# Softmax denominators of an attention block turned and summed on the vector engine instead of the tensor engine

## What is computed

```python
xn = layernorm(x)                                   # (1, 2048, 128)
q, k, v = xn @ Wq, xn @ Wk, xn @ Wv                 # 16 heads x 64
attn = softmax((q @ k.T) * 64 ** -0.5, axis=-1)
a = (attn @ v).reshape(1, 2048, 1024) @ Wo + bo
e = argmax(softmax(xn @ router_w.T))                # one expert a token
f = square(relu(xn @ expert_fc[e])) @ expert_proj[e].T
out = x + a + f
```

## Time and profile before

| | |
|---|---|
| median of 3 runs | 1392.12 us (1388.15 to 1392.15) |
| profiled execution, its own time | 1389.63 us |
| its span, first to last instruction | 1387.9 us |
| busy PE, DVE, ACT, POOL | 98%, 78%, 53%, 81% |
| DMA engines, mean busy share | 20.3% (SP's queue) |
| mean granted clock of TensorE | 0.993 of 2.4 GHz |

### The profile page before, as it was taken

One profiled execution on the slowest core, in us unless ns is written; L12 is line 12 of the kernel. 1 busy time (PEld: TensorE's weight loads), 2 busy tenths in 40 slices (PEclk: granted clock), 3 DMA queues, 4 the chain that ended last, 5 costly groups with the idle time before them and its releaser, 6 DMA issues.

```text
span 1387.9 us, 20006 instructions
## 1 busy us (share of the span) xinstructions
PE 1365.8 (98%) x6447; PEld 866.1 (62%) x6447; DVE 1078.0 (78%) x1468; ACT 735.2 (53%) x1316; POOL 1121.8 (81%) x908
## 2 busy tenths in 40 slices
PE   7899999999999999999999999999999999999997
PEld 4566666566665666666766666656667666656644
DVE  7987887786787767777777777778677777788877
ACT  4465455565464554554644645545546446556543
POOL 7779997777787877877878877879777788789995
PEclk8999999999999999999999999999999999999998
DMA  4241113220132201331113311123112231111000
GB/s 104 58 120 41 37 41 70 70 67 20 43 89 57 60 19 43 94 69 44 34 39 84 73 40 43 43 71 90 24 42 55 64 79 26 24 23 33 11 19 23
DMA packets 65255, 72.38 MB, mean 52 GB/s; under 512 B 9024, under 2 KB 38272, under 8 KB 65152
## 3 DMA queue, kind: packets, MB, share of 16 engines
q1 hardware_dynamic: 64128, 69.01, 20.3%
q0 software_dynamic: 1024, 2.10, 0.5%
HBM read 17.83 MB, written 5.11 MB: 17 GB/s over the span
## 4 chain that ended last, share of the span: by engine, by line
PE 93%; DVE 2%; POOL 1%; DMA 1%; issue 1%; SPq 1%; ACT 1%; POOLq 0%; DVEq 0%; ACTq 0%
PE OB L1116 31%; PE SB L1062 17%; PE SB L1069 16%; PE MB L1088 15%; PE XB L1153 2%; PE XB L1144 2%; PE XB L1162 2%; PE XB L1050 1%; PE XB L1043 1%; POOL acc L505 1%; DVE mx L767 1%; PE XB L1123 1%; PE XB L1125 1%; PE XB L1124 1%; DMA K<-low 1%
## 5 line engine op out<-in xcount | busy, mean ns | idle before, releaser
L505 POOL TENSOR_TENSOR acc<-acc,ex 128x512 f32<-128x512 f32 x717 | 915.9, 1304 | 99.9 <-DVE acc L790 40.4
L767 DVE TENSOR_REDUCE mx<-MB 128x1 f32<-128x512 f32 x992 | 655.9, 688 | 228.9 <-PE MB L1088 224.1
L619 ACT ACTIVATE ex<-SB 128x512 f32<-128x512 f32 x1024 | 607.2, 599 | 329.8 <-PE SB L1069 262.0
L1116 PE MATMUL OB<-ex,V 128*64 128x512 f32 x2048 | 452.7, 594 | 0.0
L1062 PE MATMUL SB<-Q,K 128*128 128x512 f32 x1024 | 421.9, 412 | 0.5 <-ACT ex L619 0.5
L1069 PE MATMUL SB<-Q,K 128*128 128x512 f32 x1024 | 399.8, 390 | 0.8 <-DMA Q<-mrow 0.8
L1088 PE MATMUL MB<-K,Q 128*128 128x512 f32 x992 | 389.1, 392 | 1.6 <-DVE mx L773 0.6
L1116 PEld LDWEIGHTS OB<-ex,V 128*64 128x64 f32 x2048 | 143.9, 137 | 284.3 <-issue 273.0
L1062 PEld LDWEIGHTS SB<-Q,K 128*128 128x128 f32 x1024 | 192.6, 188 | 96.5 <-issue 53.5
L790 DVE TENSOR_TENSOR acc<-acc,ex 128x512 f32<-128x512 f32 x179 | 205.0, 1145 | 13.5 <-ACT ex L619 1.0
L1088 PEld LDWEIGHTS MB<-K,Q 128*128 128x128 f32 x992 | 186.1, 188 | 46.7 <-DVE mx L767 5.0
(11 more groups left out here) (136 smaller groups left out, 608.8 us busy)
## 6 DMA issues: line engine op xcount, KB each, us to landing
Q<-high SPq DMA_DIRECT2D x124, 128.0 KB, 2.3
K<-high SPq DMA_DIRECT2D x112, 128.0 KB, 2.3
Q<-low SPq DMA_DIRECT2D x64, 128.0 KB, 2.4
K<-low SPq DMA_DIRECT2D x56, 128.0 KB, 2.3
w<-fc SPq DMA_DIRECT2D x23, 256.0 KB, 2.7
w<-projT SPq DMA_DIRECT2D x23, 256.0 KB, 3.1
sorted_x<-res SPq DMA_DIRECT2D x1, 1472.0 KB, 6.9
tok<-sorted_x SPq DMA_DIRECT2D x23, 64.0 KB, 1.7
```

The costliest lines, as they stand in the source:

```text
L505: pool.tensor_tensor(a[:, :], src[:, :], EX[h][ex_slot(kt)][:, :], ALU.add).then_inc(done, 1)
L619: act.activation(EX[h][ex_slot(kt)][:, :], SB[bank_of(n, 2 * kt + h)][:, :], ACT.Exp).then_inc(a_e[h], 1)
L767: dve.tensor_reduce(mx[:, m % 2, u:u + 1], MB[bank_of(m, i)][:, :], AX.X, ALU.max).then_inc(v_m, 1)
L1116: mm = pe.matmul(OB[own[h], :], V[(n // JB) % 2][:, k, own[h]], EX[h][ex_slot(k)][:, :], start=(k == 0), stop=(k == NT - 1))
```

## The change

The three jobs named leave TensorE. DVE's transpose works in squares of 32 x 32: of a 128 x 512 tile each square is turned in its place.

- Denominators. At kt 0 of block n DVE turns both `acc` tiles of block n - 1 by squares and sums each square's row (`fold_sums`), which gives `part` [128, 2 x 16]: sums over groups of 32 keys. SP's `gather_parts` brings the four groups side by side with four DMAs; DVE adds them at kt 3 (`sum_parts`), inverts 32 x 32 numbers at kt 4 (`invert`), turns them at kt 5 (`turn_row`). SP stores the result to DRAM, waits, and reads it back laid over 64 partitions a head (`spread_rd`). `normalise` waits for those DMAs.
- Maxima. `nm` is a 128 x 32 tile (8 columns used) turned by DVE at kt 12, or after the first unit in the opening (`turn_max`); `place_max` has four DMAs a head instead of one.
- Tokens. SP loads the tile with the squares already exchanged, in four DMAs instead of one; DVE turns each square at kt 3, behind `sum_parts`. `expert_up` waits for DVE.

The diff, cut to its core:

```diff
-AT_DEN, AT_KV, AT_Q, AT_WO, AT_NM, AT_T = 8, (1, 9), 5, 13, 11, 12
-AT_INV, AT_ON = 8, 10
+AT_KV, AT_Q, AT_WO, AT_NM, AT_T = (1, 9), 5, 13, 11, 12
+AT_FOLD, AT_SUM, AT_INV, AT_RD, AT_ON = 0, 3, 4, 5, 10
...
+        turned = rd
+        part, parts = sb("part", [P, SQ]), sb("parts", [SQ, P // SQ, SQ])
+        den, inv, row = sb("den", [SQ, SQ]), sb("inv", [SQ, SQ]), sb("row", [SQ, SQ])
...
                 def place_max(m):
                     k = m % QS
-                    wait(sp, a_nm, m.times(1, 1))
+                    wait(sp, v_mrow, m.times(1, 1))
                     wait(sp, g_z, 4 + 2 * QS if m.off else 4)
                     for h in range(2):
-                        copy(Q2[k][h][maxrow[h], :], mrow[h * TB:(h + 1) * TB, :], d_nm[k])
+                        row = Q2[k][h][maxrow[h], :].rearrange("o (q j a) -> o q j a", q=TB, a=SQ)
+                        for j in range(P // SQ):
+                            copy(row[:, :, j, :], mrow[j * SQ + h * TB:j * SQ + (h + 1) * TB, :], d_nm[k])
+
+                def gather_parts(n):
+                    wait(sp, v_part, n.times(2, 2))
+                    for j in range(P // SQ):
+                        sp.dma_start(parts[:, j, :], part[j * SQ:(j + 1) * SQ, :]).then_inc(d_parts, 16)
+
+                def spread_rd(n):
+                    wait(sp, v_row, n.times(1, 1))
+                    wait(sp, d_rd, n.times(32))
+                    sp.dma_start(rows_rd.rearrange("h (t b) -> (h t) b", b=SQ), row[:, :]).then_inc(d_row, 16)
+                    wait(sp, d_row, n.times(16, 16))
+                    for h in range(2):
+                        sp.dma_start(rd[own[h], :], rows_rd[h:h + 1, :].to_broadcast([DH, QB])).then_inc(d_rd, 16)
 
                 def load_tile(r):
...
-                    sp.dma_start(tok[:, :], sorted_x[bass.ds(r.place(P), P), :]).then_inc(d_tile, 16)
+
+                    rows = sorted_x[bass.ds(r.place(P), P), :].rearrange("(i a) d -> a i d", a=SQ)
+                    for j in range(P // SQ):
+                        sp.dma_start(tok[j * SQ:(j + 1) * SQ, :].rearrange("a (i b) -> a i b", b=SQ),
+                                     rows[:, :, j * SQ:(j + 1) * SQ]).then_inc(d_tile, 16)
...
                     for kt in range(NT):
                         for m in q_jobs(n, kt):
                             spread_q(m)
+                        if kt == AT_SUM - 1 and n.off:
+                            gather_parts(n - 1)
+                        if kt == AT_RD and n.off:
+                            spread_rd(n - 1)
...
                 def normalise(n):
-                    wait(pool, v_rd, n.times(2, 2))
-
+                    wait(pool, d_rd, n.times(32, 32))
...
+                def turn_max(m):
+
+
+                    wait(dve, v_nm, m.times(1, 1))
+                    if not (m.i is None and m.off == 0):
+                        old = m - 1
+                        wait(dve, d_nm[old % QS], (old // QS).times(MD, MD))
+                    dve.transpose(mrow[:, :].bitcast(F32), nm[:, :].bitcast(F32)).then_inc(v_mrow, 1)
...
+                def turn_tokens(r):
+                    wait(dve, d_tile, r.times(TD, TD))
+                    wait(dve, t_up, r.times(1))
+                    dve.transpose(tokT[:, :], tok[:, :]).then_inc(v_tok, 1)
...
-                def invert(n, part):
-                    cols = slice(part * QB // 2, (part + 1) * QB // 2)
-                    wait(dve, a_den, n.times(1, 1))
-                    dve.reciprocal(rd[:, cols], rd[:, cols]).then_inc(v_rd, 1)
+                def fold_sums(n):
+
+
+                    for h in range(2):
+                        wait(dve, sums[h][n % 2], added(n, NT - 1))
+                        if h == 0:
+                            wait(dve, g_on, n.times(1))
+                            wait(dve, d_parts, n.times(64))
+                        else:
+                            wait(dve, v_part, n.times(2, 1))
+                        dve.transpose(turned[:, :], acc[h][n % 2][:, :]).then_inc(v_turn, 1)
+                        wait(dve, v_turn, n.times(2, h + 1))
+                        dve.tensor_reduce(part[:, h * QB // SQ:(h + 1) * QB // SQ], turned[:, :].rearrange("p (t k) -> p t k", k=SQ),
+                                          AX.X, ALU.add).then_inc(v_part, 1)
+
+                def sum_parts(n):
+                    wait(dve, d_parts, n.times(64, 64))
+                    dve.tensor_reduce(den[:, :], parts[:, :, :].rearrange("b j c -> b c j"), AX.X, ALU.add).then_inc(v_den, 1)
+
+                def invert(n):
+                    wait(dve, v_den, n.times(1, 1))
+                    dve.reciprocal(inv[:, :], den[:, :]).then_inc(v_inv, 1)
+
+                def turn_row(n):
+                    wait(dve, v_inv, n.times(1, 1))
+                    wait(dve, d_row, n.times(16))
+                    dve.transpose(row[:, :], inv[:, :]).then_inc(v_row, 1)
...
-                        if kt == AT_INV and not start:
-                            invert(n - 1, 0)
-                            invert(n - 1, 1)
+                        if not start:
+                            if kt == AT_FOLD:
+                                fold_sums(n - 1)
+                            if kt == AT_SUM:
+                                sum_parts(n - 1)
+                            if kt == AT_INV:
+                                invert(n - 1)
+                            if kt == AT_RD:
+                                turn_row(n - 1)
...
+                        if has_tile(n) and kt == AT_TOK:
+                            turn_tokens(n - TILE0)
...
-                def denominators(n):
-                    take_spare(a_den, n.times(1, 1))
-                    for h in range(2):
-                        wait(pe, sums[h][n % 2], added(n, NT - 1))
-                    for h in range(2):
-                        mm = pe.matmul(XB[own[h], :], ones[:, 0:DH], acc[h][n % 2][:, :], start=True, stop=True)
-                    mm.then_inc(t_den, 1)
-
```

More of the change, by code:

```diff
@@ L169, in layer @@
         OB, XB = bank("OB"), bank("XB")
[L173 to L180, removed]
+        t_s, t_m, t_pv, t_q, t_k, t_v, t_den, t_wo = (
+            sem(f"t_{n}") for n in ("s", "m", "pv", "q", "k", "v", "den", "wo"))
+        a_e, a_o, a_q, a_k, a_w, a_v = (
+            [sem("a_e0"), sem("a_e1")], *(sem(f"a_{n}") for n in ("o", "q", "k", "w", "v")))
+        v_m, v_nm, v_mrow, v_q, v_k, v_w, v_rd, v_y = (
+            sem(f"v_{n}") for n in ("m", "nm", "mrow", "q", "k", "w", "rd", "y"))
         sums = [[sem(f"sum{h}_{k}") for k in range(2)] for h in range(2)]
@@ L193, in layer @@
         d_sort = [sem(f"d_sort{k}") for k in range(2)]
[L196 to L197 removed]
+        d_tile, v_tok, t_up, t_down, a_up, a_res, g_hid, d_res, d_back, v_back = (
+            sem(n_) for n_ in ("d_tile", "v_tok", "t_up", "t_down", "a_up", "a_res", "g_hid", "d_res",
                                "d_back", "v_back"))
@@ L203, in layer @@
         v_y0 = sem("v_y0")
+        v_turn, v_part, v_den, v_inv, v_row, d_parts, d_row, d_rd = (
+            sem(n_) for n_ in ("v_turn", "v_part", "v_den", "v_inv", "v_row", "d_parts", "d_row", "d_rd"))
         d_out = sem("d_out")
-        QD, KD = 6 * 16, 6 * 16
+        TD = (P // SQ + 2) * 16
+        QD, KD, MD = 6 * 16, 6 * 16, 2 * (P // SQ) * 16
         def unit(n, kt, h):
@@ L646, in kv @@
                                        ACT.Copy).then_inc(a_v, 1)
[L648 to L653, removed]
                 def take_o(n):
@@ L753, in one @@
                             high_q(m)
[L754 to L757, removed]
                 schedule(act, first, one, lambda: take_o(Lin(NB - 1)))
@@ L948, in one @@
                             minus_max(n + 1)
+                        if kt == AT_T and before(n, NB - 1):
+                            turn_max(n + 1)
                         if kt in AT_KV and before(n, NB - JB):
@@ L1032, in ranks @@
                     pe.matmul(XB[:, NT * E:2 * NT * E], ones[:, :], chosen, start=True, stop=True).then_inc(t_rk, 1)
-                def turn_tokens(r):
-                    take_spare(a_tok, r.times(1, 1))
-                    wait(pe, d_tile, r.times(48, 48))
-                    pe.transpose(XB[:, 0:P], tok[:, :], ident[:, :]).then_inc(t_tok, 1)
                 def expert_up(r):
                     take_spare(a_up, r.times(1, 1))
-                    wait(pe, a_tok, r.times(1, 1))
+                    wait(pe, v_tok, r.times(1, 1))
                     for c in range(NC):
@@ L1066, in low_scores @@
                     if kt == 0 and h == 0:
-                        wait(pe, d_nm[k], (n // QS).times(32, 32))
+                        wait(pe, d_nm[k], (n // QS).times(MD, MD))
                         wait(pe, d_one[par], 32)
@@ L1164, in project @@
                     mm.then_inc(t_wo, 1)
-                def turn_max(m):
-                    take_spare(a_nm, m.times(1, 1))
-                    wait(pe, v_nm, m.times(1, 1))
```

(10 more changed lines are left out.)

31 lines of the change are left out of this document (13 added, 18 removed).

## The result

The changed kernel takes 1551.8 us (1549.4 to 1554.4) against 1390.7 before: ratio 1.116, interval 1.113 to 1.119. It is 161 us slower, where 1520 was forecast and 1430 to 1600 held. The span of the profiled execution is 1552.7 us, TensorE's mean granted clock 0.951 (0.993 before).

The account below looks back on a forecast made before the run. TensorE was taken as the bound. 1389.6 - 34.5 freed + 63.6 (stall A) + 3.9 (the opening) + 69.4 (stall B) + 1 (token turn) = 1493.0; with 27 for the clock 1520 us, range 1430 to 1600.

Parts of the forecast that it names:

- The bound: Whole kernel: only TensorE has no room, busy 1278.95 of 1280 us, so its waits are added in full.
- the opening: Start of the kernel: the maxima's eight issues let TensorE go on at 48.7 instead of 44.87, 3.9 us.
- stall A: Next block's first low product: TensorE waits for maxima behind SP's eight issues, 2.05 us x 31 = 63.6 us.
- Freed, 0.92 us a block: Denominators leaving TensorE, between last maximum product and PV batch: 28.5 us over 31 blocks, of 34.5 freed in all.
- DVE at kt 0: Two turns and two reductions of 128x512 add 2.8 us, hidden under 5.05 us; the wait for POOL hidden too.
- the rival of a turn at the reciprocal's pace: DVE turns at kt 0 take 3.4 us each, 96 us more, about 1610; chance 0.03.
- Stall B: Token product: gathers behind SP's K copies delay DVE, 5.4 us x 12 blocks plus 4.6 in block 1, 69.4 us.
- The clock: TensorE's clock falls in about 8 of stall B's 13 blocks, 3.4 us each: 27 us, bounds 0 and 66.
- rival 4: Stall A costs TensorE's clock as well: 53 to 105 us more, about 1600; chance 0.09.

Follow-up runs that it names:

- the kernel before with eight DMAs: Kernel before the change, its maxima laid by eight DMAs of 32 queries instead of two of 128, turn still on TensorE: 1447.5 us, ratio 1.043.
- the denominators alone: Kernel before plus only the change's denominators' part, partial sums gathered ahead of the first K copies; maxima and tokens stay on TensorE: 1379.7 us, ratio 0.993.
- The repaired whole change: Changed kernel with partial sums gathered before the first K copies, maxima turned in kt 11 and copied before the second K copies: 1393.6 us, ratio 1.004.
- the owners' step was moved away: The denominators alone, plus tokens turned on DVE ahead of the partial sums' sum, and block 3's owners' step at kt 7, not kt 0: 1369.2 us, ratio 0.985.
- the gather ahead: Changed kernel with SP gathering the partial sums ahead of the first K copies instead of behind them: 1457.1 us, ratio 1.048.
- denominators alone, gather behind: The denominators alone, but with the partial sums gathered behind the first K copies, as in the changed kernel: 1449.5 us, ratio 1.043.

## Why the prediction was right, and where its sizes were off

**The bound.** TensorE is the bound, and its waits are added in full: right, and somewhat more than in full, as the kernel before with eight DMAs shows (0.35 us beyond each idle). Its idle time in the span went from 22.1 us to 158.7, by 136.6; the prediction's stalls and the opening were 137. That this is so close is partly chance: stall A came out 5 us smaller, and 4.7 us in block 3 were not forecast.

**Freed, 0.92 us a block.** The undisturbed blocks with the denominators alone gave 0.85 to 0.90. The repaired whole change, which sheds more, gained only 0.40 a block between the same two starts (927.0 us against 935.9), with small waits at tokens and maxima in many blocks.

**DVE at kt 0.** The turn of 128x512 takes 0.711 us where 0.69 was taken from the nearest row, and it is hidden in the middle blocks; the rival of a turn at the reciprocal's pace is out. The Trainium skill's 311 ns for a turn of 128x128 in bf16 ("VectorE: DVE Perf Modes", The three transpose paths) is near the 290 ns that this trace shows in float32. What the step missed: it judged POOL by one middle block. After indirect DMAs POOL is late, and the wait for its last add, put at nothing, stops TensorE together with the owners' step of 3.7 us behind it: 4.7 us in block 3 of the changed kernel and 6.5 in the denominators alone, but 2.2 where the owners' step was moved away.

**Stall A.** 62.4 us in 31 waits against 63.6 and 3.9. The issue was the 0.63 of the earlier trace rows less a little (0.573 median over 256); a wait is mostly 1.75 us, not 2.05. In seven blocks it is 2.1 to 3.6 us, and it is so in seven blocks with the gather ahead too, so the other stall isn't the reason; what is stays open. The kernel before with eight DMAs confirms the term without the rest of the change.

**Stall B.** 65.5 us in 12 waits against 64.8, 4.6 in block 1 against 4.6. Its mechanism was right to the queue; the experiments add that it doesn't need the tokens, which only lengthen it from 3.5 us to 5.4.

**The clock** is the term that was mis-sized: 27 us forecast, some 50 measured. The prediction put a fall behind about 8 of the 13 long idles at 3.4 us each, and nothing behind the short ones of stall A. The second of these is the step that failed. In windows of 6 us from the end of each idle, the granted clock falls short of full by 26.9 us of work behind the 13 long idles, by 2.8 behind the one in block 3, and by 25.1 behind 15 of the 30 idles of stall A. So the 27 us for stall B came out by luck: the clock fell behind all 13, not 8, and a fall cost 2.1 us on average (1.4 to 2.9), not 3.4, because part of the slow stretch lay in the idle itself. What the forecast lacked is rival 4, given 0.09: its mechanism was real, at 25 us instead of 53 to 105.

Windows of the changed kernel (stretch, length, busy us of PE, PEld, DVE, ACT, POOL, clock), first around the long idle before 687.44, then around one of 2.28 us that ended at 665.69. The last line of each is its window of 6 us:

```profile
684.00:688.00 4.00, 0.56 (x2) 0.59 (x3) 1.28 (x4) 0.00 (x0) 2.95 (x3) 0.76 0.11 21
688.00:692.00 4.00, 4.00 (x14) 3.42 (x14) 1.42 (x3) 1.53 (x3) 1.04 (x1) 0.50 0.02 4
692.00:696.00 4.00, 4.00 (x17) 3.25 (x16) 2.82 (x6) 2.79 (x6) 2.22 (x2) 0.88 0.06 15
...
687.44:693.44 6.00, 6.00 (x19) 5.14 (x20) 2.67 (x5) 1.99 (x4) 2.15 (x2) 0.54 0.01 3
```

```profile
664.00:668.00 4.00, 2.31 (x5) 1.49 (x5) 0.69 (x1) 0.80 (x2) 3.48 (x3) 0.70 0.13 28
668.00:672.00 4.00, 4.00 (x17) 1.29 (x18) 3.50 (x6) 0.40 (x1) 0.00 (x0) 0.87 0.67 186
...
665.69:671.69 6.00, 6.00 (x21) 2.71 (x23) 3.91 (x6) 1.19 (x2) 1.93 (x2) 0.72 0.51 136
```

The deficits give 1.9 + 4 + 1.0 = 6.9 us at half clock around the long idle, 1.3 of them before its end, and 2.4 + 1.0 = 3.4 behind the short one. So this long idle cost 2.8 us of work, and a short one behind which the clock fell costs 1.7. These deficits are a little too high as a price, since a 512-column product starts every 0.43 us at half clock and every 0.227 at full, not quite twice: 55 us of them are some 50 of time. The same instructions kept TensorE busy 1394.0 us in the changed kernel and 1344.7 in the version with both repairs; those 49 us agree, but hold what the waits add at full clock as well. The rule of the Trainium skill that idle between bursts drops the clock ("TensorE: Matmul & The Clock Gate", HAM oscillation) held behind every long idle here and behind half of the short ones, and the time it gives is nearer than the sum without it: 1493 stands 59 us below what was measured.

Taken together: -32 for what TensorE sheds (0.87 x 31 and 0.1 x 54), 62.4, 65.5, 4.6 and 4.7 for the waits, some 50 for the clock give 155 of the 165 us of span. If each of the 45 waits cost 0.35 us beyond its idle, as in the kernel before with eight DMAs, that would be 16 more, an estimate: it covers the rest and overshoots by 6, which is how well these terms close.

## What to carry to other kernels

When an engine at 98% is relieved, count what the relief asks of the queues: here 16 more transfers a block (six for the maxima, four and three for the denominators, three for the tokens) replaced products worth 1 us, and one issuing queue at 0.6 us a transfer made 128 us of waits. Read the order in that queue before its load, which is low; a transfer behind another job's copies waits for that job's data too. And whatever stops TensorE for 1.75 us or more is to be priced with the clock that it may lose; in the one case where it could be read, a stop cost 0.35 us more than its idle.

## What the runs showed of the hardware

- An issue on SP costs 0.57 to 0.63 us (medians) whether it moves 512 bytes or 128 KB within SBUF; the issues of a load of tokens in four pieces took 1.74 to 2.96 us instead of 0.33.
- A stop of TensorE costs more than its idle: 1.69 us for 1.3 us idle, over 22 blocks at full clock (the kernel before with eight DMAs).
- Idle times and the clock, in blocks 1 to 31. With idles of 1.3 us (eight DMAs in the kernel before) it fell behind none of 28; the two falls there followed longer ones, of 3.0 and 2.1 us. With 1.75 to 2.75 us it fell behind 8 of 29 (gather ahead) and 14 of 29 (changed kernel), with 3.5 to 3.8 us behind 9 of 12 (denominators alone, gather behind), with 5.4 us behind all 12. It isn't a matter of length alone: equal idles did and didn't cost it.
- A DVE operation with two SBUF inputs and 184 columns took 3.7 us at kt 0 beside POOL's unbroken adds, in six kernels. In the kernel before, where POOL issued DMAs beside it, and at kt 7 in four others it took 0.33 to 0.95 us (0.38 where the adds were 0.14 us apart). One with a single input, the turn, took 0.71 us beside the same adds. The Trainium skill ("SBUF — State Buffer", Who interferes with whom) names this contention; that the wait can last to the end of a run of POOL's adds, and not only of one of them, the rows here add.
